# Attention outputs in two rounded passes over stacked context halves, and a new memory layout

## The reference, cut to what matters

```python
scores = jnp.einsum('bhqd,bhkd->bhqk', q, k) * scaling      # 16 heads, causal
probs = jax.nn.softmax(scores, axis=-1)
out = jnp.einsum('bhqk,bhkd->bhqd', probs, v)               # v = latent @ Wv per head, rank 64
return out.reshape(b, s, H * V_DIM) @ o_proj_w.T
```

## Time and profile before

| | |
|---|---|
| median of 3 runs | 861.79 us (859.61 to 862.86) |
| profiled execution | 859.85 us, span 858.1 us |
| mean granted PE clock | 0.989 |
| busy in the span | PE 793.7, DVE 581.5, ACT 390.6, POOL 251.3 us |
| DMA | 112.78 MB |

### The profile page before, as it was taken

How to read it: one execution, slowest core, us unless ns; L and a number is a source line. 1 busy time by engine, 2 the same in 40 slices (tenths; PEclk the granted TensorE clock), 3 DMA queues, 4 the chain that set the end, 5 groups by cost and what they waited for, 6 DMA issues and landing times.

```text
span 858.1 us, 16693 instructions
## 1 busy us (share of the span) xinstructions
PE 793.7 (92%) x4717; PEld 671.0 (78%) x4718; DVE 581.5 (68%) x1440; ACT 390.6 (46%) x883; POOL 251.3 (29%) x342
## 2 busy tenths in 40 slices
PE   8998879999999999999899999988799799999997
PEld 7887667668788777777699999877787677777786
DVE  4324687887888878778626666388866277777656
ACT  1335546555556665665214444122233156666531
POOL 2004346433433232230346666311104300000061
PEclk9999999999999999999999999999989999999999
DMA  7349941000000000000769999475634211111031
GB/s 213 101 109 388 410 163 47 27 27 27 27 20 28 21 21 20 20 34 1 253 224 350 358 366 370 169 294 196 224 112 155 74 31 49 49 49 49 26 90 64
DMA packets 62793, 112.78 MB, mean 131 GB/s; under 512 B 17936, under 2 KB 35344, under 8 KB 61584
## 3 DMA queue, kind: packets, MB, share of 16 engines
q1 hardware_dynamic: 51744, 87.55, 29.8%
q0 software_dynamic: 7680, 21.51, 7.0%
q10 hardware_dynamic: 3312, 3.02, 1.0%
HBM read 68.26 MB, written 43.78 MB: 131 GB/s over the span
## 4 chain that ended last, share of the span: by engine, by line
PE 64%; DVE 15%; issue 12%; ACT 3%; POOL 2%; DMA 2%; SPq 1%; DVEq 0%; ACTq 0%; POOLq 0%
PE scores L1530 8%; PE scores L1532 8%; PE scores L1531 8%; PE scores L1750 7%; PE probsT_ps L1639 5%; PE acc_ps L1666 4%; PE scores L1761 3%; PE misc_ps L1654 3%; PE misc_ps L1652 3%; DVE xT_lo L993 3%; PE probsT_ps L1884 3%; PE acc_ps L1941 2%; DVE neg_max L987 2%; PE misc_ps L1538 2%; POOL xd_d L674 2%
## 5 line engine op out<-in xcount | busy, mean ns | idle before, releaser
L723 ACT ACTIVATE area<-scores,neg_max 128x128 f32<-128x128 f32 (+7 forms) x128 | 94.8, 742 | 81.3 <-DVE neg_max L987 80.6
L987 DVE TENSOR_REDUCE neg_max<-scores 128x1 f32<-128x128 f32 (+7 forms) x128 | 95.8, 751 | 21.7 <-PE scores L1615 21.3
L1639 PE MATMUL probsT_ps<-ident,area 128*128 128x128 f32 x552 | 83.1, 275 | 10.6 <-DVE xT_lo L993 10.0
L1666 PE MATMUL acc_ps<-area,sgd 128*128 128x256 f32 x248 | 77.4, 394 | 13.8 <-DVE x_rows L1010 12.7
L993 DVE TENSOR_TENSOR xT_lo<-probsT_ps,xT_hi 128x512 fp32r<-128x512 f32 x92 | 62.9, 687 | 28.5 <-ACT xT_hi L730 27.0
L621 POOL DMA_INDIRECT xe_d<-x_rows,send_i x64 | 63.9, 999 | 60.1 <-DVE send_i L1099 48.5
L1639 PEld LDWEIGHTS probsT_ps<-ident,area 128*128 128x128 f32 x552 | 62.5, 141 | 22.4 <-issue 17.0
L651 POOL DMA_INDIRECT ye_d<-area,home_i x64 | 61.4, 959 | 45.4 <-issue 42.7
L1530 PE MATMUL scores<-kT_hi,weff_hi 128*128 128x512 f32 (+3 forms) x172 | 66.3, 385 | 4.2 <-DVE xT_lo L1426 1.9
L1750 PE MATMUL scores<-area 128*96 128x128 f32 x512 | 66.6, 273 | 0.4 <-DVE area L1181 0.4
L730 ACT ACTIVATE xT_hi<-probsT_ps 128x512 fp32r<-128x512 f32 x92 | 54.2, 593 | 26.7 <-PE probsT_ps L1639 26.5
(11 more groups left out here) (264 smaller groups left out, 1925.0 us busy)
## 6 DMA issues: line engine op xcount, KB each, us to landing
area<-gate_up SPq DMA_DIRECT2D x32, 384.0 KB
xe_d<-area SPq DMA_DIRECT2D x8, 1088.0 KB, 11.5
area<-xe_d SPq DMA_DIRECT2D x32, 272.0 KB
ye_d<-area SPq DMA_DIRECT2D x8, 1024.0 KB, 15.9
area<-w SPq DMA_DIRECT2D x8, 1024.0 KB, 7.1
area<-ye_d SPq DMA_DIRECT2D x8, 1024.0 KB, 4.9
area<-down SPq DMA_DIRECT2D x32, 192.0 KB, 5.7
area<-w SPq DMA_DIRECT2D x8, 512.0 KB, 7.7
```

Source lines behind the costliest of these rows:

```text
L723: act.activation(row_of(n)[:, 0:L], score_bank(n)[:, 0:L], ACT.Exp, bias=neg_max[:, n % 4:n % 4 + 1], accum_out=rsum[:, s, k:k + 1]).then_ ...
L987: dve.tensor_reduce(neg_max[:, n % 4:n % 4 + 1], score_bank(n)[:, 0:(n // HEADS + 1) * P], AX.X, ALU.max, negate=True).then_inc(max_ready, 1)
L1639: last = pe.transpose(seat_of("block", b)[:, i * P:(i + 1) * P], row_of(QUAD * G + i)[:, k * P:(k + 1) * P], ident[:])
L1666: pe.matmul(out_of(n), ctxT[:, G % 2, i * P:(i + 1) * P], wvo[:, h * HID:(h + 1) * HID], start=True, stop=True).then_inc(out_ready, 1)
```

## The change

Rounded operands allow a faster matmul, but lose low bits. The new output is two rounded passes into the same PSUM place. The first multiplies all 128 rows of the rounded context (`ctx_hi`) with the rounded weights (`wvo_hi`). The second multiplies `ctx_both` with `wvo_both`: rows 0 to 63 hold what rounding left of the first 64 context rows, against rounded weights; rows 64 to 127 hold the rounded first 64 context rows, against what rounding left of the weights.

For this, `wvo_copy` on DVE becomes three operations per pair of heads. ACT copies the context twice, once rounded and once in fp32 (64 rows, into the place of q that is used up), and issues a DMA that moves 64 rounded rows to partitions 64 to 127. POOL makes the remainder (`rest_of_ctx`). The outputs, their additions and the variance of a tile move one slot later; one more output and one more addition stand after the last slot.

The memory is laid out anew: `area2` goes, `area5` holds the two weight tensors and later `gathered` and `w2`, `area6` the contexts and later the shared down weights. x is read straight into `x1`. The expert down weights and the recurrence's weights lie in `area1`, so that the last two `w1` are loaded only after the recurrence. `w2` and the shared down weights are first copied from HBM to HBM, 4 MB and 1 MB, on SP's queue behind the zero writes, and loaded from there.

```diff
-        area2 = sb("area2", [P, 4 * HC * T])
...
-        area4 = sb("area4", [P, 6144])
-        cutA2, cutA3, cutB4 = carve(area2), carve(area3), carve(area4)
-        cutB3, cutC2, cutC3, cutD3, cutD4 = (carve(a) for a in (area3, area2, area3, area3, area4))
+        area4 = sb("area4", [P, 4096])
+        area5 = sb("area5", [P, 2 * HEADS * HID], f32r)
+        area6 = sb("area6", [P, 4, BANK], f32r)
+        cutA3, cutB4 = carve(area3), carve(area4)
+        cutB3, cutC3, cutD3, cutD4 = (carve(a) for a in (area3, area3, area3, area4))
...
-        x_in = cutA2(TILES, HID)
-        prob_rows = [area2[:, 2048 + 1024 * m:3072 + 1024 * m] for m in range(6)] + [
-            area4[:, 1024 + 1024 * m:2048 + 1024 * m] for m in range(ROWS_KEPT - 6)]
-        xT_in = cutA2(HC, T)
-        sq = cutA2(TILES, RANK)
-        keys = cutA2(TILES, P)
+        prob_rows = [area4[:, 1024 + 1024 * m:2048 + 1024 * m] for m in range(3)] + [
+            area3[:, 1024 + 1024 * m:2048 + 1024 * m] for m in range(ROWS_KEPT - 3)]
...
+        wkb = cutA3(HEADS, RANK)
...
-        wkb = cutA3(HEADS, RANK)
...
-        wvo = cutA3(HEADS * HID)
+        xT_in = cutA3(HC, T)
+        sq = cutA3(TILES, RANK)
+        keys = cutA3(TILES, P)
...
+        wvo_hi, wvo_both = area5[:, 0:HEADS * HID], area5[:, HEADS * HID:]
...
-        ctxT = sgd
...
+        ctx_hi, ctx_both = area6[:, 0:2, :], area6[:, 2:4, :]
...
-        zero_rows = area4[:, 6144 - T:]
+        zero_rows = sgd[:].rearrange("p u n -> p (u n)")
...
-        dn_w = cutB4b(RING, HID)[0:I0]
+        dn_w = area1[0:I0, 4096:4096 + RING * HID].rearrange("p (e n) -> p e n", e=RING)
...
-        no_home = area3[:, 7168:7168 + E0]
-        mine = area3[:, 7168 + E0:7168 + E0 + 4 * TOP0].rearrange("p (a e k) -> p a e k", a=2, e=2)
-        home = area3[:, 7168 + 2 * E0:7168 + 2 * E0 + 2]
...
-        gathered = cutC2(2, TOP0, HID)
-        w_c = cutC2(6, HC, HID)
-        wo_c = cutC2(2, HC, HID)
+        no_home = cutB4(E0)
+        mine = cutB4(4 * TOP0).rearrange("p (a e k) -> p a e k", a=2, e=2)
+        home = cutB4(2)
...
+        gathered = area5[:, 0:2 * TOP0 * HID].bitcast(f32).rearrange("p (u k n) -> p u k n", u=2, k=TOP0)
+        cutC1 = carve(area1[:, 6 * HC * 2 * I1:])
+        w_c = cutC1(6, HC, HID)
+        wo_c = cutC1(2, HC, HID)
...
-        w2_s = area2
+        w2_s = area5[:].bitcast(f32)
...
-        sh_g, sh_u, sh_d = cutD4(HC, SH), cutD4(HC, SH), cutD4(SH // P, HID)
+        sh_g, sh_u = cutD4(HC, SH), cutD4(HC, SH)
+        sh_d = area6[:].bitcast(f32).rearrange("p u (c n) -> p (u c) n", n=HID)
...
-            sp.dma_start(x_in[:], x.rearrange("(t p) n -> p t n", p=P)).then_inc(ld_x, 16)
+            sp.dma_start(x1, x.rearrange("(t p) n -> p t n", p=P)).then_inc(ld_x, 16)
...
+            sp.dma_start(w2_d.rearrange("e (p a) n -> p e (a n)", p=P), w2.rearrange("e (p a) n -> p e (a n)", p=P)).then_inc(copied, 16)
+            sp.dma_start(sh_down_d.rearrange("(p a) n -> p (a n)", p=P),
+                         sh_down.rearrange("(p a) n -> p (a n)", p=P)).then_inc(copied, 16)
...
+            sp.wait_ge(ctx_lo, GROUPS - 2)
...
             loads_sh = ((sh_g, sh_gate.rearrange("(c p) f -> p c f", p=P)), (sh_u, sh_up.rearrange("(c p) f -> p c f", p=P)),
-                        (sh_d, sh_down.rearrange("(c p) n -> p c n", p=P)))
+                        (sh_d, sh_down_d.rearrange("(c p) n -> p c n", p=P)))
+            sp.wait_ge(copied, 32)
             for t in range(TILES):
...
                     load_results(t + 2)
-                if t + 2 < E1:
+                if t + 2 < 6:
                     load_w1(t + 2)
...
             for e in range(E1):
+                if e >= 6:
+                    load_w1(e)
                 sp.dma_start(w2_s[:, e * I1 * HID // P:(e + 1) * I1 * HID // P].rearrange("p (c n) -> p c n", n=HID),
-                             w2[e].rearrange("(c p) n -> p c n", p=P)).then_inc(ld_w2, 16)
+                             w2_d[e].rearrange("(c p) n -> p c n", p=P)).then_inc(ld_w2, 16)
             xd_v = xd_d.rearrange("(i p) n -> p i n", p=P)
...
+            def ctx_of(G):
+
+                t, g = divmod(G, SETS)
+                return qT.rearrange("p (h t) -> p h t", h=HEADS)[0:RANK, g * QUAD:(g + 1) * QUAD, t * P:(t + 1) * P]
+
+            def rest_of_ctx(G):
+                pool.wait_ge(ctx_copied, 2 * G + 2)
+                pool.tensor_tensor(ctx_both[0:RANK, G % 2, :].rearrange("p (h n) -> p h n", h=QUAD), ctx_of(G),
+                                   ctx_hi[0:RANK, G % 2, :].bitcast(f32).rearrange("p (h n) -> p h n", h=QUAD),
+                                   ALU.subtract).then_inc(ctx_lo, 1)
+
...
+                if i == 0 and 0 <= G - 2 < GROUPS:
+                    rest_of_ctx(G - 2)
+                if SETS + 2 <= G < GROUPS and (G % SETS, i) == (2, 1):
+                    rstd_of(tile_of(G) - 1)
...
-                if SETS + 2 <= G < GROUPS and (G % SETS, i) == (2, 0):
-                    rstd_of(tile_of(G) - 1)
...
                     act.wait_ge(out_ready, QUAD * (G - 1))
-                act.copy(ctxT[:, G % 2, :], ctx_ps[:]).then_inc(ctx_copied, 1)
+                t, g = divmod(G, SETS)
+                act.copy(ctx_hi[:, G % 2, :], ctx_ps[:]).then_inc(ctx_copied, 1)
+                act.copy(qT.rearrange("p (h t) -> p h t", h=HEADS)[0:RANK, g * QUAD:(g + 1) * QUAD, t * P:(t + 1) * P],
+                         ctx_ps[0:RANK, :].rearrange("p (h n) -> p h n", h=QUAD)).then_inc(ctx_copied, 1)
+                act.wait_ge(ctx_copied, 2 * G + 1)
+                act.dma_start(ctx_both[RANK:, G % 2, :].bitcast(f32), ctx_hi[0:RANK, G % 2, :].bitcast(f32)).then_inc(ctx_moved[G % 2], 16)
...
+                two = bass.ds(2 * m * HID, 2 * HID)
                 hold(dve, wvo_ps, 2 * m + 2)
-                dve.tensor_copy(wvo[:, bass.ds(2 * m * HID, 2 * HID)], misc[:]).then_inc(wvo_done, 1)
+                dve.tensor_copy(wvo_hi[:, two], misc[:]).then_inc(wvo_done, 1)
+                dve.tensor_copy(wvo_both[0:RANK, two], misc[0:RANK, :])
+                hold(dve, wvo_done, 2 * m + 1)
+                dve.tensor_tensor(wvo_both[RANK:, two], misc[RANK:, :], wvo_hi[RANK:, two].bitcast(f32),
+                                  ALU.subtract).then_inc(wvo_done, 1)
...
-                dve.scalar_tensor_tensor(x1[:, t, :], out_of(n), rinv[:, s, k:k + 1], x1[:, t, :] if h else x_in[:, t, :],
+                dve.scalar_tensor_tensor(x1[:, t, :], out_of(n), rinv[:, s, k:k + 1], x1[:, t, :],
...
-                behind = n - 1 - 2 * QUAD
+                behind = n - 2 - 2 * QUAD
                 if 0 <= behind < TILES * HEADS:
...
                 if routed:
-                    if at == (2, 0):
+                    if at == (2, 1):
                         attention_variance(t)
...
+            add_head(TILES * HEADS - 2)
...
-                    pe.wait_ge(wvo_done, i)
+                    pe.wait_ge(wvo_done, 2 * i)
...
-                        pe.wait_ge(ctx_copied, G)
+                        pe.wait_ge(ctx_copied, 2 * G)
...
-                pe.wait_ge(ctx_copied, G + 1)
+                pe.wait_ge(ctx_copied, 2 * G + 1)
...
                 h = n % HEADS
-                pe.matmul(out_of(n), ctxT[:, G % 2, i * P:(i + 1) * P], wvo[:, h * HID:(h + 1) * HID],
-                          start=True, stop=True).then_inc(out_ready, 1)
+                heads = slice(h * HID, (h + 1) * HID)
+                pe.matmul(out_of(n), ctx_hi[:, G % 2, i * P:(i + 1) * P], wvo_hi[:, heads], start=True, stop=False)
+                pe.wait_ge(ctx_lo, G + 1)
+                pe.wait_ge(ctx_moved[G % 2], 16 * (G // 2 + 1))
+                pe.matmul(out_of(n), ctx_both[:, G % 2, i * P:(i + 1) * P], wvo_both[:, heads],
+                          start=False, stop=True).then_inc(out_ready, 1)
...
-                if 0 <= G - 2 < GROUPS:
-                    output(QUAD * (G - 2) + i)
+                if n > 2 * QUAD:
+                    output(n - 1 - 2 * QUAD)
...
+            output(TILES * HEADS - 1)
```

More of the change, by code:

```diff
@@ L212, in build @@
         ye_d = nc.dram_tensor("ye_d", (SLOTS + T * TOP0, HID), f32).ap()
+        w2_d = nc.dram_tensor("w2_d", (E1, I1, HID), f32).ap()
+        sh_down_d = nc.dram_tensor("sh_down_d", (SH, HID), f32).ap()
         banks = [ctx.enter_context(nc.psum_tensor(f"scores{u}", [P, 2 * BANK], f32)) for u in range(2)]
@@ L252, in build @@
         last_sends = sem("last_sends")
+        ctx_lo, copied = sem("ctx_lo"), sem("copied")
+        ctx_moved = [sem(f"ctx_moved{u}") for u in range(2)]
         consts0, route_step, exp0, weight_done = (
@@ L1600, in _ @@
             pe.wait_ge(weff_f32, HEADS)
-            pe.wait_ge(wvo_done, PAIRS)
+            pe.wait_ge(wvo_done, 2 * PAIRS)
             def scores(n):
```

## The result

The kernel after takes **901.1 us** (median of 4 runs, 899.8 to 903.0) beside 862.3 us for the kernel before (4 runs, 859.6 to 863.3): ratio 1.047, 95% interval 1.044 to 1.050. The sign was forecast, the size was not: 880 us was the figure, and 895 the top of the range. The profiled execution spans 899.3 us against 858.1, so 41.2 us are to be found.

The account below looks back on a forecast made before the run. Attention was taken as bound by a loop through PE (the fullest engine), ACT and DVE. The terms 3.7 + 1.8 + 9 + 4 = 18.5 us on 859.85 gave 878.4, or 880 us on the median's scale, range 858 to 895.

Parts of the forecast that it names:

- Projections: Head projections: DVE's wvo_copy becomes three operations and delays PE, +3.7 us (2 to 5).
- Attention net: Attention: ACT's added work less the output saving, +4.8 us in tiles 5 to 7, -3 in 0 to 4, sum +1.8.
- ACT's insertion: ACT at each context copy: a second PSUM copy (0.58 us) and a DMA issue (0.34), +0.92 before exp.
- the shorter output: Output matmul: two rounded passes take 0.31 us instead of 0.43, saving 0.12 each (0.05 to 0.19) over 128.
- the row of 0.34: Profile row giving a DMA issue 0.34 us in ACT's queue; the forecast counted it rather than dropping it.
- The DMA of the moved half: Early attention: landing near t+6.8 after the copy at t stalls PE in eight groups, +9 us (0 to 22).
- I take half: Of some 18 us gross DMA stalls only half, +9 us, counts, because DVE catches up after each stall.
- Tail: End of attention: the last output waits for the DMA beside SP's expert weight loads, +4 us (2.9 to 6.1).
- Nothing for POOL, loads, new places: POOL's subtraction, weight loads before the last stage (13 us cover) and tensors at new places: no added time.
- Rival A: TensorE is what counts: added ACT work hides, 0.19 us saved per output, -14 in all, 848 us; chance 0.12.
- B: The small DMA is hidden anyway, ACT's queue not slowed by SP's: 871 us, down to 860; chance 0.2.
- D: The DMA queues behind the bulk, latency over 8 us: near 910 us, 895 with a halfway latency; chance 0.18.

Follow-up runs that it names:

- e6: Kernel after, but the second pass reads the rounded context in all 128 rows, with no DMA issued or waited for; ratio 1.008 to the kernel before.
- b2: Kernel after with one wvo copy, one context copy, no POOL subtraction, no DMA; two passes of rounded context and weights; ratio 0.994 to the kernel before.
- b4: Kernel after with one wvo copy, one context copy, no POOL subtraction, no DMA; four rounded passes per output; ratio 1.003 to the kernel before.
- e5: Kernel after, but the second pass reads the rounded context in 128 rows without waiting for the DMA, which ACT still issues; ratio 1.015 to the kernel before.
- e1: Kernel after, but the second pass reads only POOL's 64 rows without waiting for the DMA, still issued; 900.4 us, ratio 1.047 to the kernel before.
- e2: Kernel after, but the second pass reads only POOL's 64 rows and ACT issues no DMA; ratio 1.039 to the kernel before.
- f1: Kernel after with TensorE repeating the first pass (40 times, then 20) before its DMA wait in the first five groups; ratio 1.039 to the kernel before.
- e4: Kernel after with the HBM copies and the zero writes of ye_d and xd_d held until tile 6; ratio 1.034 to the kernel before.
- t3: Kernel after with three 128-row passes and no DMA; ACT copies the context once in fp32, POOL makes both halves; ratio 1.004 to the kernel before.
- n1: Kernel after with one rounded context copy, no POOL subtraction or DMA; second pass uses the weights' rest in 128 rows; ratio 0.996 to the kernel before.

## Why the prediction was wrong in size

- **Projections, +3.7 (2 to 5): right.** The first context copy came 4.0 us later; over all kernels with the three operations 3.9 to 5.0, but for one at 6.7. With two operations of 128 rows it was 0.5 to 2.1, with one -0.3 and 1.7.
- **Attention net, +1.8 (-14 to +18): 11.3, in the bounds and wrong in the value.** It was 0.76 x 12 + 0.45 x 20 = 18 us for ACT's insertion, less 0.36 x 12 + 0.6 x 20 = 16 for the shorter output. The insertion was sized well as a sum: 10.0 for the second copy with POOL's part and 6.8 for the issue (from group 0 on), 16.8; in tile 7 PE's wait grew by 0.40 with the copy (e6: 1.04) and by another 0.28 with the issue (1.32). The failed term is the 16: of the shorter output 5.5 us came through (b2), and b4 shows the same rate, 8.4 us for 30 us more of PE's work (from -5.5 to +2.9 between groups 0 and 30). It failed in tiles 0 to 4: from group 0 to 20 b2 gains 3.2 us on the kernel before where 12 were set down, so that the -3 of these tiles came out as +8.5 (e5); tiles 5 to 7, set at +4.8, came to +2.9 by group 30. PE is full, but in these kernels only about a quarter of what is taken off it or added comes through. That rate is no constant: of the 27 us that the 64-row passes add, 20 to 21.5 came through (e1 - e5, e2 - e6), and no run tells why. The Trainium skill (DMA: Bandwidth & Descriptors, "Issuing engines are not separate DMA queues") says that the time to initiate a DMA is usually small relative to the DMA itself. So it is in the trace, 0.47 us beside 2.2 to 7.1, but by that rule the issue would have been left out, and it cost 6.8; the row of 0.34 was the better guide.
- **The DMA of the moved half, +9 (0 to 22): 17.9 from group 0 on. The failed step is "I take half".** The gross figure of 18 was right, and that was luck, since its factors were not. The landing was 6.7 to 7.1 us instead of 5.6, and the second pass began at t+7.4 to 7.9 instead of 6.8; PE began the group's first output at t+5.0 in group 1, and at t+3.9 in group 2 where filled passes kept its clock up (f1), near the t+4.06 that I had read off; and five groups stalled, not eight, the first of them with no cover at all (6.67). The halving rested on DVE catching up after each stall. PE's waits for DVE between the copies of groups 0 and 7 did shrink, from 9.7 us to 7.9, 1.8 instead of 9, and of the 18.5 us of stalls 17.9 stayed. From one copy to the next it took 9.9 to 11.3 us, through issue, landing, the group's first output and what follows it; that work which DVE finishes sooner isn't on that path is my reading, and f1, where PE came sooner and waited longer, fits it. Not every stall stays whole: against e5 the first, of 6.67 us, cost 4.5, and the next four, of 2.6 to 3.1 under a lowered clock, 3.0 to 4.1 each; e4, with 7.7 us of stalls far apart, lost 4.7.
- **Tail, +4 (2.9 to 6.1): 7.6.** The landing was 6.3 instead of up to 5.6, so the output came 7.1 us after the copy instead of 0.6; beside the wait the granted clock was 0.50 from 455 to 460 us. Without a DMA the tail still costs 5.1 (e6: 9.0 to 14.1), where PE waits 1.23 us for POOL, and 3.0 in b2, which has neither a second copy nor POOL's part; the last head, which now stands alone, is the likely reason for the 3.0, and no run isolates it. The sum had these 3 to 5 at nothing.
- **Nothing for POOL, loads, new places: right.** In attention PE waits for the DMA and never for POOL. From the experts' start to the end 0.8 us were added.

Sum: 4.0 + 11.3 + 17.9 = 33.2 at group 30, -0.4 to group 31, 7.6 and 0.8: 41.2. Of the 22.7 us that the sum was short, 9.5 are in the attention net, 8.9 in the halved stall and 3.6 in the tail. Rival A (0.12) fell with PE's small share; B fell in early attention; D named the right place and a wrong mechanism: the time came near its figure (895 to 910), but the latency stayed below the 8 us from which it was to decide. The Trainium skill (DMA: Bandwidth & Descriptors, "Queues, rings and completion order") says that each DMA engine goes round the queues at packet granularity; the trace agrees: on ACT's queue 128 KB landed in 7 us, while on SP's 1 MB took 17.3 and 4 MB took 27.6.

## What to carry to other kernels

Before a moved or copied half is put between two matmuls, find the path from one group to the next with the latency in it. Where group after group stalled here, the stalls stayed almost whole (17.9 of 18.5 us), and the half taken off for engines that catch up was wrong; full DMA engines, harmless to the kernel before, set the price of every small DMA on that path. A second copy on an engine with half its time free cost up to 10 us, since exp stood behind it in the loop; in t3, where POOL does that work, 5.6 us of it came back, and n1 leaves it out.

## What was not expected of the hardware

- A pass over 64 rows between passes over 128 cost 0.52 us for the pair instead of 0.31: its weight load did not run beside the pass before it. Of these 27 us for PE 20 to 21.5 reached the time of attention.
- A DMA of 128 KB inside SBUF landed after 6.7 to 7.1 us beside full DMA engines (350 to 406 GB/s), after 6.3 beside the expert loads, and after 2.2 (median) otherwise.
- The granted clock was 0.50 for the five us after a stall of 6.67 us. With the clock kept up by idle passes the time was the same, 1.039 beside 1.040, though the groups up to the fifth came 0.7 to 3.4 us sooner.
- **Open:** between the copies of groups 30 and 31, b2, b4 and n1 lose 4.4 to 5.5 us. In all three PE stands still there for reasons that the profile doesn't show, 1.1 and 1.3 us in n1, 1.0 and 1.3 in b2, and in b4 3.2 us in one piece, after which the clock is at the lower level (0.50 from 412 to 416 us in b2):

```profile
422.39 0.79 PE L1681 MATMUL misc_ps<-xT_hi 128*128 128x512 f32 x1 [3.15 <-issue]
```

SP's expert loads, whose wait these three kernels change, begin only behind that (412.99 in b2), so they are not the cause; no run tells what is.
